# Last NF4 group: the first half's down product ahead of the second half's gate and up, and the fourth norm's first turns among the last down products

## The reference, cut to what matters

```python
x1 = x + o                                    # NF4 attention-like part
g = lin_lora(x1, gate);  u = lin_lora(x1, up) # 512 -> 1792
h = silu(g) * u
x = x + x1 + lin_lora(h, down)                # 1792 -> 512; x1, too, starts from the third norm
xn = layernorm(x)                             # the fourth norm
xq = nvfp4_qdq(xn[:, up_reorder_index])       # permuted channels, then quantized by blocks of 16
...                                           # gate, up, silu, quantize, down, and a low-rank product
```

## Time and profile before

| what | us |
|---|---|
| median of 3 runs | 830.16 |
| lowest and highest | 827.44, 838.89 |
| the profiled execution | 835.99 |
| its span, first to last instruction | 834.7 |
| TensorE busy in it | 729.9 (87%) |
| VectorE busy | 568.5 (68%) |
| ScalarE busy | 441.5 (53%) |
| mean granted TensorE clock | 0.951 of full |

### The profile page before, as it was taken

The page is one execution under the profiler, slowest core; times in us unless marked ns, Lnnn a source line. Parts: engine busy times, 40 slices in busy tenths (PEclk is TensorE's granted clock), DMA queues, the critical chain, the costliest instruction groups (busy, mean ns, idle before and its releaser), DMA issues.

```text
span 834.7 us, 11304 instructions
## 1 busy us (share of the span) xinstructions
PE 729.9 (87%) x4136; PEld 542.3 (65%) x4136; DVE 568.5 (68%) x1083; ACT 441.5 (53%) x573; POOL 190.1 (23%) x176
## 2 busy tenths in 40 slices
PE   1798765989999998889998999778999799959998
PEld 1565522656767666657665777565777588947886
DVE  4789966662687888689897974667453443467773
ACT  4778777465785868687666511264322221224542
POOL 0214000021354452436553442122001200000000
PEclk9999968999999999999998999988899899988999
DMA  8737679765386776658745200212001210200001
GB/s 281 217 114 213 197 259 284 249 217 192 119 241 195 218 230 217 216 180 251 235 144 151 77 35 26 64 41 65 9 0 38 60 53 21 76 10 13 25 26 39
DMA packets 56039, 110.55 MB, mean 132 GB/s; under 512 B 9888, under 2 KB 20800, under 8 KB 55984
## 3 DMA queue, kind: packets, MB, share of 16 engines
q1 hardware_dynamic: 42560, 78.43, 29.4%
q10 hardware_dynamic: 9040, 17.30, 6.5%
q0 software_dynamic: 4384, 14.09, 6.0%
HBM read 91.65 MB, written 18.15 MB: 132 GB/s over the span
## 4 chain that ended last, share of the span: by engine, by line
PE 56%; DVE 20%; ACT 8%; issue 8%; DMA 6%; SPq 1%; ACTq 1%; DVEq 0%
PE bank L1118 14%; PE bank L1119 13%; PE bank L1120 13%; PE bank L1225 3%; ACT hot L1524 3%; DVE hot L1770 2%; DMA wide_buf<-in_down_flat 2%; DVE bank L1796 2%; DVE x L1893 2%; PE bank L1413 2%; ACT c L1483 2%; PE bank L1267 1%; PE bank L1238 1%; DVE q_a L1843 1%; DMA codes<-c 1%
## 5 line engine op out<-in xcount | busy, mean ns | idle before, releaser
L1524 ACT ACTIVATE hot<-rep,levels 128x2048 f16<-128x2048 f16 x96 | 193.6, 2057 | 16.5 <-ACT c L1483 11.0
L1118 PE MATMUL bank<-zt_h,w_h 128*128 128x512 f32 (+1 forms) x232 | 93.3, 402 | 2.6 <-DVE zt_l L1881 2.0
L1120 PE MATMUL bank<-zt_h,w_l 128*128 128x512 f32 (+1 forms) x232 | 91.4, 394 | 0.0
L1119 PE MATMUL bank<-zt_l,w_h 128*128 128x512 f32 (+1 forms) x232 | 91.2, 393 | 0.0
L1118 PE MATMUL bank<-w_h,xq_h 128*128 128x512 f32 (+1 forms) x192 | 75.6, 394 | 5.8 <-DVE w_l L1912 3.5
L1225 PE MATMUL bank<-hot,diag 128*32 128x512 f16 x1160 | 78.2, 399 | 2.3 <-ACT hot L1524 2.2
L1119 PE MATMUL bank<-w_l,xq_h 128*128 128x512 f32 (+1 forms) x192 | 73.3, 382 | 0.0
L1120 PE MATMUL bank<-w_h,xq_l 128*128 128x512 f32 (+1 forms) x192 | 72.9, 380 | 0.0
L2037 POOL TENSOR_TENSOR q_a<-q_a,q_m 128x384 f32<-128x384 f32 (+3 forms) x34 | 35.7, 1051 | 107.9 <-DVE q_m L1664 106.9
L1225 PEld LDWEIGHTS bank<-hot,diag 128*32 128x32 f16 x1160 | 26.1, 98 | 45.3 <-issue 23.9
L1118 PE MATMUL bank<-w_h,at_h 128*128 128x512 f32 x112 | 48.1, 430 | 8.0 <-DVE x L1893 5.2
(11 more groups left out here) (222 smaller groups left out, 1686.4 us busy)
## 6 DMA issues: line engine op xcount, KB each, us to landing
rep<-codes SPq DMA_DIRECT2D x58, 512.0 KB
codes<-c SPq DMA_DIRECT2D x29, 256.0 KB
raw<-in_codes_gu_t ACTq DMA_DIRECT2D x14, 512.0 KB
sc<-in_scales_gu_t SPq DMA_DIRECT2D x56, 128.0 KB
raw<-in_codes_attn_t ACTq DMA_DIRECT2D x8, 512.0 KB
raw<-in_codes_down_t ACTq DMA_DIRECT2D x7, 512.0 KB
sc<-in_scales_down_t SPq DMA_DIRECT2D x28, 128.0 KB
wide_buf<-in_gate_flat SPq DMA_DIRECT2D x5, 512.0 KB, 4.2
```

The costliest lines, as they stand in the source:

```text
L1118: PE.matmul(psum, lh, rh, start=first, stop=False, **kw)
L1119: PE.matmul(psum, lh, rl, start=False, stop=False, **kw)
L1120: return PE.matmul(psum, ll, rh, start=False, stop=last, **kw)
L1524: S.activation(hots[plan.slot[hot_ring(t), (t, m)]][:], codes_in_place(t), ACT.Relu, bias=bias, scale=slope).then_inc(sem("ramp_act"), 1)
```

## The change

The pair ("d", 6, 0) is taken out of the order and put in front of the last two, so that it reads ..., gu 6 0, d 5 1, d 6 0, gu 6 1, d 6 1. The split of weight tile 57, `perm` and the first row gathers go with it, since the loop puts them in front of this pair. The first `next(norm4)` now stands behind gu 6 1, and the second inside d 6 1, behind `dn_mm 6, 5` and ahead of `dn_add 6, 5`. `known` of the first half, with its square root, goes with d 6 0 and so stands ahead of the Silus of gu 6 1.

```diff
@@ -649,6 +649,8 @@
     for g in range(NG):
         nxt = g + 1 < NG
         order += [("d", g, 0)] + [("gu", g + 1, 0)] * nxt + [("d", g, 1)] + [("gu", g + 1, 1)] * nxt
+    order.remove(("d", NG - 1, 0))
+    order.insert(-2, ("d", NG - 1, 0))
     rows = [[(name, t) for name in ("up", "gate") for t in range(f0 // P, (f0 + w + P - 1) // P)] for f0, w in CHUNKS]
     p.rows = rows
 
@@ -689,12 +691,14 @@
             p.sends("perm_in", "perm", 2)
             p.sends("lr_in", "lr", 2)
             next(first_fetch)
-        for _ in (gate_up if what == "gu" else down)(g, half):
+        for i, _ in enumerate((gate_up if what == "gu" else down)(g, half)):
             side_nf4.step()
             side_fp4.step()
+            if (what, g, half, i) == ("d", NG - 1, 1, 1):
+                next(norm4)
         through.add((what, g, half))
-    for _ in range(normed):
-        next(norm4)
+        if (what, g, half) == ("gu", NG - 1, 1):
+            next(norm4)
     p.turn4 = p.turns % 2
     p.inherit("turn4", [("turn", 2, p.turn4), ("code", 2, 0), ("code", 2, 1), ("turn", 2, 1 - p.turn4)])
     p.inherit("main4", [("main", 3, 0), ("main", 3, 1), ("main", 3, 2), ("lora", 1, 0)])
```

## The result

The changed kernel took 831.51 us (median of 20 runs, 827.35 to 835.44), the kernel before 836.35 (20 runs, 827.44 to 842.27). The ratio is 0.9949, 95% interval 0.9931 to 0.9967: 4.3 us faster, with 2.8 to 5.8 in the interval; by the medians 4.8. In a second session the ratio was 0.9925 (0.9897 to 0.9952). The time lay in the range given; the gain was about twice the 2.4 us forecast, and it came by other terms. The profiled execution took 829.33 us, against 835.99 before.

What follows compares the result with a forecast made beforehand. TensorE was taken as the bound, through waits and half clock between 511.05 and 552.80. A full-clock gain of 5.65 us less 3.2 for low clock gave 2.4, from median 830.16 to 827.8 us; range 821.5 to 834.

Steps and rivals of the forecast that it cites:

- E + 2.4: First early turn, inside the wait behind the second half's gate and up: runs 2.4 us after their end, 532.41.
- E + 4.4: Start of dn_mm 6, 4 behind the second turn: 4.4 us after gate and up end, at 536.8.
- rival 3: ScalarE's tables: a switch costs more than its load, as the page has it; gain 1.5 us, 828.7; chance 0.05.
- price of 0.9 us: ScalarE's table switches: an estimate by the skill page, first switch covered and second not, makes the sum 0.9 us worse.
- rival 2: Index transfer ahead of VectorE's permutation: each microsecond over 4.68 costs one; at 9.4, 2.3 us slower, 832.5; chance 0.12.
- I take both: 3.2 us: Clock: a low stretch behind the waits before the fourth tile and dn_mm 6, 4, 1.6 us apiece, nothing hiding it.
- rival 1: Clock: fewer low stretches behind the two long waits; gain 4.0 us with one, 5.65 with none; chance 0.30.
- a shift won before 552.80 is carried on: TensorE from 552.80 to 568.4: busy without a gap at full clock, 15.60 us, so earlier gains are kept.
- `phase`, 1.49 us: Ahead of pprod 0: the many waits of phase still cost 1.49 us, putting pprod 0 at 544.4.
- Nothing again, with 0.3 us to spare: Second added table load, before the second half's root: runs about 543.6 to 544.9 beside the last add, costing nothing.
- Covered by 1.2 us: norm 4, needed by the successor of pprod 1: ends at 548.2, asked for at 549.4.
- 5.65 less 2.3: Start of pprod 1: 552.80 to 547.15 gains 5.65 us at full clock; 2.3 was the old run's visible half clock.

Runs made afterwards that it cites:

- e3: Changed kernel with VectorE's making of the permutation behind the adds of down 6, 0; ratio to before 0.9911.
- e6: Changed kernel with the second early turn behind dn_mm 6, 4 and not ahead of it; ratio to before 0.9924.
- e5: Changed kernel with the split of weight tile 57 ahead of down 5, 1, not behind its last add; ratio to before 0.9968.
- e8: Changed kernel with ten and nine matmuls that nobody reads in TensorE's two long waits; ratio to before 0.9936.
- e11: Kernel before with unread matmuls in its waits: eleven behind gate/up, fourteen ahead of turn 2, seven ahead of quantized x's first turned tile; ratio to before 0.9938.
- e1: Changed kernel with the new group order kept but the turns put back behind all down products; ratio to before 0.9986.
- r1: Kernel before, unedited, run once more with a profile of another execution; ratio to before 0.9988.
- e4: Changed kernel with one small square root on ScalarE behind tsplit 1, to load the root's table there; ratio to before 0.9929.
- r2: Changed kernel, unedited, run once more in a second session; ratio to before 0.9925.
- e12: Changed kernel with ten and nine unread matmuls in its two long waits, seven ahead of quantized x's first turned tile; ratio to before 0.9901.
- e2: Kernel before, old group order, with the fourth norm's first turns behind dn_mm 6, 4 and 6, 5; ratio to before 0.9970.
- e7: Changed kernel with the edits of e3, e4, e5 and e6 together; median 821.21 us, ratio to before 0.9814.
- e9: Changed kernel with the edits of e3, e4 and e6, without e5's early split; 821.89 us, ratio to before 0.9821.
- e10: e7 with nine unread matmuls in the wait behind gate/up of the second half; 823.17 us, ratio to before 0.9821.

## Why the prediction was right or wrong

Right were most times of TensorE's rebuilt timeline: `dn_mm 6, 0` at 512.78 (measured 512.80); the fourth tile at 520.13 (519.83, the index landing 0.3 earlier); the end of gate and up at 532.41 (532.27); turn 0 at E + 2.4 (2.38) and turn 1 ahead of `dn_mm 6, 4`, E + 4.4 (4.7, 0.3 of it by the clock); and e3 and e6 show that the permutation and that turn are what holds these places. The first table load was hidden, and the drain of about 1.38 us that the Trainium skill ("ScalarE: Activation LUTs", What ACT_TABLE_LOAD costs) puts behind a load was again not there (526.62 behind 525.33 plus 1.28): rival 3 falls. Its price of 0.9 us does not come out of the prediction's terms either: with the drain the table would be ready at 546.3, 1.1 us behind the root's input, and the cover of 1.2 us given to `norm 4` would have held that. The end on the other side (rival 2) did not come in the change, but in e5.

Wrong were three terms of the sum, and with them the size of the gain.

1. "I take both: 3.2 us." This is the step that failed most. The prediction charged a low stretch to each long wait and held both for uncovered ("nothing hiding it"). The measured charge is 1.1 us on the down tiles and 0.3 on the turn ahead of them: no stretch behind the first wait, one behind the second, and e8 shows that 1.1 is all that filling wins in M. It was rival 1's case (chance 0.30). That the old stretch at 525 was covered was seen; that the clock's charge in the old kernel reached beyond 552.80 was not. The statement that "a shift won before 552.80 is carried on" left out the low stretches behind it, 10.2 us before and 3.4 after in both pairs of profiles, worth 2.9 us; by e11 they are clock.
2. "`phase`, 1.49 us." It cost at most 0.2 us: `pprod 0` started 0.45 us behind the last down matmul, where the next matmul starts 0.23 behind. In e1, where TensorE comes to `phase` out of a wait, it took 1.67 us again. It took 1.5 to 1.7 us in the four profiles in which TensorE had waited at the turn just ahead (before, r1, e1, e11), and next to nothing in the twelve in which the down products ran up to it. By itself this won nothing, as the next point shows.
3. "Nothing again, with 0.3 us to spare", of the second table load, and "Covered by 1.2 us", of `norm 4`. The load stood behind the variance and not ahead of it, and made the root 1.3 us late. And the cover was counted to the end of `norm 4`, while turn 4 waits for its bank, which comes free only behind `tsplit 2` and `tdiff 2`, 1.2 us later (550.08 and 551.27). So there was no cover, and turn 4 waited 1.83 us. e4 removes 1.3 of it, and the 0.55 left is this chain. What sets the third product is the chain from the last down product through add, statistics, root, `norm 4`, split and `tdiff 2`: from the last down matmul's start it took 7.94 to 7.96 us in all seven profiles with the late load (changed, r2, e3, e5, e6, e8, e12), though TensorE's own work there is 6.1 us (7.95 less the wait of 1.83), and 6.67 or 6.68 in e2, e4, e7 and e9, where no load stood in it (7.18 in e10). As an estimate from these, TensorE would still have waited there with `phase` at its old price (6.1 and 1.3 are 7.4). The other loads (524.04, 506.72 in the changed kernel) ran far ahead of their roots, and why this one did not was not tried.

By its own measure the forecast put the end of the down products at 546.1 (542.9 and the clock's 3.2) and the third product at 553.1 (550.35 for `pprod 1` and a step). They came at 544.08 and 551.80: 2.0 us too pessimistic on the way there, by the clock, and 0.7 too optimistic behind. That this half cancels is luck. With the clock held at full the forecast had 5.65 less 2.3, so 3.35 us; e11 and e12 differ by 2.3 us. That this is close to the 2.4 of the forecast is luck too, since the forecast meant 5.65 less 3.2. The rest of the 4.3 to 4.8 us is clock: 1.5 in M, and in the profiles up to 2.9 behind it. The runs without a profile had a higher mean clock too (0.953 against 0.947), but where in the kernel is not on record, and whether the change brings about the part behind M each time stays open: e4, with the changed order, did not have it.

The median forecast (827.8) started from three runs at 830.16; twenty have 836.35. So the measured 831.51 lies 3.7 us above the forecast time though the gain was larger than forecast.

## What to carry to other kernels

An order change that makes data early pays only with the consumer moved too: by M, e1 alone gave nothing and e2 about a quarter (1.0 of 3.8 us). List every instruction that waits on one engine and stands ahead of what another needs (here VectorE's index, ScalarE's table, TensorE's second turn), and move these together, since one at a time they may even lose. Follow a cover to the last reader of the bank that TensorE waits for, and not only to the next instruction. Where TensorE waits two or three microseconds in several places, first see what the waits cost in clock behind them: 32 unread matmuls in the old kernel's waits were worth as much as the reordering.

## What the runs showed of the hardware

- The idle before the fourth tile, 2.6 to 3.0 us, was followed by full clock in both profiles of the changed kernel and in e1, e4 and e6, but in e11, 2.76 us there were followed by a fall (532.7). One of 2.76 behind gate and up was followed by a fall in both profiles of before and in e2. In e5 the clock fell in the 5.18 us wait itself. From 500 to 610, in all sixteen profiles, each fall began inside a wait of TensorE or at most 1.7 us behind one, but most waits brought none.
- The activation behind a table load starts 0.01 to 0.02 us after its end (525.33, 546.41, 591.56). The first root's load ran 12 to 19 us ahead of its activation, the second root's only behind what that waits for, in all seven profiles with the late load (546.41 in the changed kernel).
- The index of 2 KB to each of 128 partitions took 3.8 to 4.3 us from issue to use in the eleven profiles in which VectorE waited for it and the last store of down weights had been issued over 2 us before (3.9 in the changed kernel, 4.2 in before), with row gathers beside it each time, and 6.1 in e5.
